# Masking two of four key tiles with a VectorE minimum in place of TensorE mask products

## What is computed

```
xn  = layernorm(x)
Q, K, V = relu(xn Wq + bq), relu(xn Wk + bk), relu(xn Wv + bv)      # 16 heads of 16
scores  = Q K^T / 4;  masked where the key row sums to 0, and where key > query
out = softmax(scores) V + xn, normalised, * gamma + beta
ffn = the two best of 8 experts (gated, 256 -> 512 -> 256) + one shared expert
x + out + ffn
```

## Time and profile before

| | |
|---|---|
| median of 3 runs | 1978.3 us (1972.72 to 1979.48) |
| the profiled execution | 1995.76 us, of which the span is 1994.0 us |
| mean granted TensorE clock | 0.965 |
| PE busy | 1809.1 us (91%) |
| DVE busy | 1249.0 us (63%) |
| ACT busy | 1107.1 us (56%) |
| POOL busy | 1169.0 us (59%) |
| iterations that attend one batch and find maxima of the next | 15, from 118 us to 988 us |

### The profile page before, as it was taken

The page is one execution under the profiler, slowest core; times in us unless marked ns, Lnnn a source line. Parts: engine busy times, 40 slices in busy tenths (PEclk is TensorE's granted clock), DMA queues, the critical chain, the costliest instruction groups (busy, mean ns, idle before and its releaser), DMA issues. The chain is left out here.

```text
span 1994.0 us, 37209 instructions
## 1 busy us (share of the span) xinstructions
PE 1809.1 (91%) x13046; PEld 1331.4 (67%) x13046; DVE 1249.0 (63%) x2528; ACT 1107.1 (56%) x2114; POOL 1169.0 (59%) x1437
## 2 busy tenths in 40 slices
PE   3589999998899999989879999999999988899998
PEld 2345555555555555555437888888888887788887
DVE  6777887678778787757626545445454444466666
ACT  5246566666555656655446666666666666333332
POOL 4354557656556765653436777777777776444443
PEclk9689999999999999999879999999999999999999
DMA  3756676776677677667536566666666664444443
GB/s 89 126 99 111 111 127 140 145 129 142 138 139 135 143 138 134 134 125 156 177 134 214 189 193 218 210 212 198 193 218 210 215 202 158 127 148 150 154 149 103
DMA packets 232322, 310.89 MB, mean 156 GB/s; under 512 B 18986, under 2 KB 197300, under 8 KB 225972
## 3 DMA queue, kind: packets, MB, share of 16 engines
q1 hardware_dynamic: 219892, 275.49, 55.2%
q0 software_dynamic: 12288, 33.57, 5.9%
HBM read 210.12 MB, written 98.86 MB: 155 GB/s over the span
## 5 line engine op out<-in xcount | busy, mean ns | idle before, releaser
L653 ACT ACTIVATE pT<-st_ps 128x512 f32<-128x512 f32 x682 | 372.1, 557 | 364.7 <-PE st_ps L1271 310.6
L931 DVE TENSOR_REDUCE mx<-s_ps 128x1 f32<-128x512 f32 (+3 forms) x704 | 434.1, 637 | 195.8 <-PE s_ps L1245 185.2
L1968 PE MATMUL gu<-xc,w_up_h 128*128 128x512 f32 (+1 forms) x1120 | 337.2, 384 | 11.6 <-POOL w_up_l L1652 7.8
L1243 PE MATMUL s_ps<-k_aug,q_aug 97*128 97x512 bf16 (+3 forms) x1024 | 289.7, 316 | 31.3 <-DVE mx L931 28.2
L1831 DVE TENSOR_TENSOR hf<-sil,gu 128x512 f32<-128x512 f32 (+1 forms) x220 | 143.8, 654 | 277.7 <-ACT sil L1750 270.3
L1269 PE MATMUL st_ps<-q_aug,k_aug 99*128 99x512 bf16 (+1 forms) x992 | 277.3, 312 | 21.4 <-ACT pT L653 20.5
L1834 DVE TENSOR_TENSOR hid_l<-hf,hid_h 128x512 fp32r<-128x512 f32 (+1 forms) x220 | 173.0, 787 | 147.6 <-ACT hid_h L1752 134.4
L482 POOL DMA_INDIRECT expert_rows<-xrow,slot x128 | 125.4, 980 | 210.3 <-DMA q_aug<-neg_scr 119.5
L1968 PEld LDWEIGHTS gu<-xc,w_up_h 128*128 128x128 f32 x1120 | 204.5, 189 | 56.0 <-POOL w_up_l L1652 9.4
L1750 ACT ACTIVATE sil<-gu 128x512 f32<-128x512 f32 (+1 forms) x220 | 123.9, 563 | 202.0 <-PE gu L1968 185.2
L1752 ACT ACTIVATE hid_h<-hf 128x512 fp32r<-128x512 f32 (+1 forms) x220 | 133.1, 605 | 174.3 <-DVE hf L1831 168.9
(11 more groups left out here) (262 smaller groups left out, 4040.5 us busy)
## 6 DMA issues: line engine op xcount, KB each, us to landing
early_raw<-in_L_ffn_w_dram SPq DMA_DIRECT2D x60, 512.0 KB
w_raw<-in_L_ffn_w_dram SPq DMA_DIRECT2D x57, 512.0 KB, 5.7
part_scr<-parts SPq DMA_DIRECT2D x64, 384.0 KB, 9.6
q_aug<-part_scr SPq DMA_DIRECT2D x192, 128.0 KB
k_aug<-part_scr SPq DMA_DIRECT2D x192, 128.0 KB
early_raw<-expert_rows SPq DMA_DIRECT2D x34, 512.0 KB
expert_results<-yo SPq DMA_DIRECT2D x32, 512.0 KB, 3.3
x_sb<-in_L_attn_x_dram SPq DMA_DIRECT2D x16, 512.0 KB
```

The source lines that it names most:

```text
L653: fn(pT[:, j % 2, h:h + heads, 0:w], unit_view(column_bank(b, u), heads, w), ACT.Exp).then_inc(exp_done, 1)
L931: vec.tensor_reduce(mx[:, q, h:h + heads], unit_view(s_ps[(NU * b + u) % 3], heads, keys), AX_X, ALU.max).then_inc(s_max, 2)
L1243: mm(v[:, n], q_aug[par][0:ROWS_S, h0 + n, P * q:P * (q + 1)], k_aug[par][0:ROWS_S, h0 + n, 0:keys], start=True, stop=False)
L1968: last = mm(gu[m % 2][:, a, 0:width(n)], w_up[wpar][x][:, a, c, P * m:P * (m + 1)], xc[par][:, y, c, 0:width(n)], start=k == 0, stop=k == ...
```

## The change

Column scores of tiles 0 and 1 (`BOUNDED`) no longer get the mask product. In its place DVE takes, after the exponential, the least of the diagonal block of `pT` (128 partitions, 4 heads x 128 columns of fp32, one instruction for a group and tile) and of a constant `limit`: 2^127 where key <= query, 0 elsewhere. `weigh` of these tiles waits for that minimum instead of the exponential. `bound` stands in DVE's queue right behind the row maximum of the step after the tile's last unit, and before all else of that step; `weigh` stands in the step after that. `limit` is made once at the start, by one memset and one select on POOL.

```diff
+        limit = sb("limit", [P, P])
+        BOUNDED = (0, 1)
...
+            gp.memset(limit[:], INFINITE).then_inc(consts, 1)
+            await_(pool, consts, 14)
+            gp.affine_select(out=limit[:], in_=limit[:], compare_op=ALU.is_ge, fill=0.0, base=0,
+                             pattern=[[1, P]], channel_multiplier=-1).then_inc(consts, 1)
...
+            def bound(b, g, j):
+
+                await_(dve, exp_done, NU * b + last_unit[g, j] + 1)
+                own = pT[:, j % 2, :, 0:P]
+                vec.tensor_tensor(own, own, limit[:].rearrange("p (o n) -> p o n", o=1).to_broadcast([P, GH, P]),
+                                  ALU.min).then_inc(bounded, 1)
...
+                    if attend:
+                        for g in range(GROUPS):
+                            for j in BOUNDED:
+                                if last_unit[g, j] + 1 == s:
+                                    bound(i, g, j)
...
-                    mm(v[:, n], k_aug[par][0:ROWS_ST, h, P * j:P * (j + 1)], q_aug[par][0:ROWS_ST, h, P * j:S],
-                       start=True, stop=False)
-                    last = mm(v[:, n, 0:P], identb[:], cmask[:, 1], start=False, stop=True)
+                    last = mm(v[:, n], k_aug[par][0:ROWS_ST, h, P * j:P * (j + 1)], q_aug[par][0:ROWS_ST, h, P * j:S],
+                              start=True, stop=j in BOUNDED)
+                    if j not in BOUNDED:
+                        last = mm(v[:, n, 0:P], identb[:], cmask[:, 1], start=False, stop=True)
...
-                await_(pe, exp_done, NU * b + last_unit[g, j] + 1)
+                if j in BOUNDED:
+                    await_(pe, bounded, len(BOUNDED) * (GROUPS * b + g) + j + 1)
+                else:
+                    await_(pe, exp_done, NU * b + last_unit[g, j] + 1)
```

More of the change, by code:

```diff
@@ L200, in attention_phase @@
          rd_ready, mask_part, mask_sum, ones_ready, chain_rest, chain_neg, chain_norm, chain_quot, q_ready, normed,
-         both_ready, ranks_ready, ranks_read, routes_ready, table_ready, chain_route, chain_table, filled) = [sem(n) for n in (
+         both_ready, ranks_ready, ranks_read, routes_ready, table_ready, chain_route, chain_table, filled, bounded) = [sem(n) for n in (
              "w_in rows_in consts consts_dve w_cut rw_ps rw_cut setup_sem bcol_ps bcol_ok pads x_in a_ready "
@@ L207, in attention_phase @@
              "q_ready normed both_ready ranks_ready ranks_read routes_ready table_ready chain_route chain_table "
-             "filled").split()]
+             "filled bounded").split()]
         qk_written, aug_loaded, nm_ready, neg_ps, neg_out, neg_stored, neg_loaded, row_in, scattered = (
@@ L471, in _ @@
             gp.memset(tri, 1.0).then_inc(consts, 1)
-            await_(pool, consts, 13)
+            gp.memset(limit[:], INFINITE).then_inc(consts, 1)
+            await_(pool, consts, 14)
+            gp.affine_select(out=limit[:], in_=limit[:], compare_op=ALU.is_ge, fill=0.0, base=0,
+                             pattern=[[1, P]], channel_multiplier=-1).then_inc(consts, 1)
             gp.affine_select(out=tri, in_=tri, compare_op=ALU.is_ge, fill=0.0, base=-1, pattern=[[1, P]],
@@ L759, in _ @@
                 setup_mark(vec.memset(region[:, e:e + 1], float(STRIDE * e)))
-            await_(dve, consts, 14)
+            await_(dve, consts, 16)
             vec.tensor_copy(trib[:], tri)
```

## The result

The change makes the kernel slower: 2135.4 us (2129.3 to 2143.4) against 1978.9, a ratio of 1.080 with an interval of 1.077 to 1.084. The sign was forecast and the size was not: 156 us instead of 60, and outside the range, whose upper end was 2105.

What follows compares the result with a forecast made beforehand. Neither PE nor DVE was taken to bound the iteration alone. Place costs less PE's saving gave 2.9 us, plus 1.1 for waits on POOL 4.0 an iteration; over 15 iterations 60 us, so 2038 us, range 1985 to 2105.

Steps and rivals of the forecast that it cites:

- (a) to (e): Added cost of the eight minima, place by place, in one iteration: 0.7 + 0.3 + 1.2 + 1.2 + 0.6 us.
- (f): PE time saved by dropped mask products where no wait takes it: 1.4 us an iteration at most, 1.1 taken.
- (g): Minima held by POOL's elementwise work: 0 to 4.1 us or more an iteration, about a quarter taken, 1.1.
- (a): Step 40 through step 6, DVE nearly gapless: minima (3, 1) and (0, 0) lengthen the run, together 0.7 us.
- (b) to (e): Minima an iteration: (0, 1) 0.3 us; (1, 0), (1, 1) 1.2; (2, 0), (2, 1) 1.2; (3, 0) 0.6.
- (e): Minimum at (3, 0), where PE is full and there is no slack: 0.6 us an iteration.
- even: Rival: minima cost what the products save, 0.24 us each, as PE's waits replace one another: 1978 us; chance 0.06.
- hidden: Rival: minima cost nothing in DVE's idle time and PE keeps its 1.9 us an iteration: 1949 us; chance 0.09.
- lock: Rival: waits on POOL met in full, 8.4 us an iteration, 126 us in all, 2104 us; chance 0.18.

Runs made afterwards that it cites:

- the run with the reduction and no products: The changed kernel with a 512-element DVE row reduction (one SBUF operand, dead output) in place of the minimum, `weigh` waiting for it: ratio 1.0395.
- the link alone: The kernel before, mask products kept, plus at each minimum's place a 128x1 DVE memset that waits for the exponentials and that `weigh` waits for: ratio 1.0134.
- the run with the reduction and the products kept: The kernel before, mask products kept, plus a 512-element DVE row reduction (one SBUF operand) at each minimum's place, `weigh` waiting for it: ratio 1.039.

## Why the prediction was wrong

The sign was right and the mechanism in the main, the sum was 4.0 us an iteration and the measured loss is 10.4 (156.5 / 15). By its terms, from the runs:

| | predicted | measured |
|---|---|---|
| link and length, terms (a) to (e) | 4.0 | 5.2 (1.039, 1.0395) |
| products saved, (f) | -1.1 | 0 (1.0007, and 1.0793 against 1.080) |
| waits on POOL, (g) | +1.1 | 5.3 (1.080 less 1.0395) |

**(g) is the step that failed.** It had two parts, how long the minima are held and what a held microsecond costs. The first was bounded rightly: the excess over an undisturbed 0.68 us, summed over the eight places and averaged over 15 iterations, is 2.7 us, within 0 to 4.1. The four places of the text carry 2.4 of it (0.2 at (1, 1), 0.3 at (2, 0), 0.9 at (2, 1), 1.0 at (3, 0)), and (1, 0), which it didn't list, 0.3. In iteration 7, from which the bound was read, the minima are held 4.0 us in all: there the upper bound came out nearly whole. So taking a quarter of it was the first mistake: POOL's share of the iteration gave no reason to believe that the queues would shift into the gaps.

The second was to price a held microsecond at one microsecond or less, "as the longer waits let DVE's later lateness be paid at the same time". With the link 2.7 us of holding cost 5.3 us; without it 3.5 us of holding cost 2.0 (1.0253 less 1.0105). The changed kernel beside the run with the reduction and no products shows where the rest goes. This is the row of that run over the 14 iterations:

```profile
120.70:988.20 867.50, 720.83 (x6097) 419.25 (x6095) 664.83 (x1460) 489.23 (x935) 474.70 (x707) 0.97 0.61 122
```

The changed kernel takes 80.7 us longer here. For the same 6097 products PE is busy 30.2 us more, at the lower clock (121 us at half speed for 54), and idle 50.5 us more, for 41 us of holding in the stretch. So a held microsecond costs about 1.2 us of PE's idle time, and the rest goes with PE's slower work. (The changed kernel's profile is of its slowest run, at a clock of 0.947 where the three others had 0.953 or 0.954, so the part of the clock is rather too large here.) The rows at 648 to 653 us show both: while the minimum is held, PE stands at `weigh`; when it comes free, PE needs 2.8 us, at half clock, for `weigh` and the next row scores, and DVE stands for 2.25 of them. The prediction has no term for the clock. It read 1.00 in one iteration and concluded that "nothing here is a matter of clock"; before the change that is so in that iteration, after it it isn't. How much of the time would come back at full clock is not shown: the run with products and minimum has the higher clock and the same time.

On the rule quoted in (g) from the Trainium skill, page "SBUF — State Buffer", section "SBUF: two separate sides": the trace agrees on the main point, that a DVE instruction with two SBUF inputs and a GpSimd instruction exclude each other: the minimum ends 0.55 us behind POOL's product, and POOL's next takes 2.22 us for 1.89. The reduction with one input is never held (at most 0.69 us over 128). The bound worked out by that rule, 4.1 us, would have been the better (g), yet still short of 5.3. Against the row of 3.66 us, no minimum of the 15 iterations sat out more than one of POOL's products (2.31 us at most); one of the last batch did, with 4.38.

**(a)** held at its first place only. At (0, 0) PE waits 1.27 us at `weigh` and then 1.28 for `y` where it waited 2.90: one wait for the other, as forecast. The rows are those of PE at the head of the iteration:

```profile
600.96 1.07 PE L1304 MATMUL oT<-pT,v_aug 128*32 128x512 f32 x8 [1.27 <-ACT v_aug L720]
603.85 0.66 PE L1232 MATMUL misc<-identf,xn 128*128 128x128 f32 x4 [1.28 <-DVE y L959]
```

(The releaser named in the first is not the last one: the minimum runs from 600.17 to 600.86, and ACT's `v_aug` was done at 600.28.) But (3, 1) was priced at 0.6 us, its length, because DVE would be the only engine that matters there. PE waits 2.14 us for it, and steps 38 to 43, in the mean over 14 iterations from PE's first row scores of step 38 to those of the next iteration's step 0, went from 6.6 to 11.7 us, to 9.9 with the reduction and to 8.3 with the link alone. As I read it, PE had run ahead of DVE through these steps before and paid once, at `y`. The link makes it pay at (3, 1) too, and DVE then has no finished row scores waiting for it.

**(f)** was wrong in kind. 0.06 us for each product is right as PE's time (27.0 us less in 448 products between the two runs with the reduction), but an iteration in which PE and DVE are each idle a good part of the time, and in turn, is paced by the loop between them. The text itself says in its first paragraph that neither bounds the iteration, and then credits PE's savings nonetheless.

**(b) to (e)** together are near: with (a), 4.0 forecast and 5.2 measured. That is luck in part. In the run with the reduction and the products kept, an iteration grew by 5.0 us in the profile, 3.3 of them in the steps 38 to 43, where (e) and (3, 1) were to cost 1.2, and 1.7 in all the others, where 2.8 were forecast. The last iteration, put at 0, is not quite that: its minimum of 4.38 us lies in the part of the span that grew by 5.0. The rival "even" is refuted by every run with the link; "hidden" by the link alone. The rival "lock" was the right case: its 8.4 us come nearest to the 10.4. It has the waits on POOL in full, and what it lacks is that they cost more than their length.

## What to carry to other kernels

Before crediting an engine with saved time, ask whether it is full where the saving lies: removing 1.9 us of PE's work from a 57 us iteration gained nothing, as it turned into waiting and, in one of the comparisons, into a slower clock. A new wait across engines costs its lateness even if the work behind it is 59 ns long (1.8 us an iteration here), and it raises the price of what delays the waited-for instruction: its bare length cost 1.4 us an iteration without the wait and 3.4 with it, 3.5 us of holding cost 2.0 without and 2.7 us cost 5.3 with it, a part of that through the clock. In a stretch in which POOL does elementwise work, price a DVE instruction with two SBUF operands by POOL's running instruction, or give it one operand.

## What the runs showed of the hardware

- A DVE instruction with two SBUF operands can sit out several of POOL's: 3.66 us over three in the kernel before; a minimum of the last batch 4.38 us in the changed one and 8.43 us, over six of POOL's products, in the run with tile 0 only, against 0.69 undisturbed. A row reduction of the same elements beside the same POOL work never took more than 0.70 us, nor did a product of 512 elements with one operand in PSUM. POOL is held too: 2.22 us for 1.89.
- PE's clock fell after a short idle time: 2.3 us idle, then 0.52 of full speed for 3.5 us, in which `weigh` took 1.93 instead of 1.06 us. Idle times of 2.18 us (before 641.37) and 2.14 us (before 657.87) in the same iteration were not followed by it. Of the 34 idle times of PE from 1.9 to 3.7 us in the 14 iterations, 24 were: 1.5 us after their end the clock's records have half speed. Half-speed time in the 14 iterations rose from 46 to 121 us with the change.
- Useful products can be free. With the minimum in place, 27 us more of PE work in 14 iterations left the time as it was, at a higher clock (0.96 for 0.94).
